# Causal mask of the attention's row maxima: from TensorE products to a fused VectorE instruction

## What is computed

```python
Q, K, V = x @ W_Q.T, x @ W_K.T, x @ W_V.T          # x after layer norm; 16 heads of 16
attn = jnp.einsum('bhqd,bhkd->bhqk', Q, K) * scale
attn = jnp.where(causal, attn, -jnp.inf)
probs = jax.nn.softmax(attn, axis=-1)
y = jnp.einsum('bhqk,bhkd->bhqd', probs, V)
x = x + y @ W_O.T
x = x + ffn(layernorm(x))                          # shared expert and 2 of 16 experts a token
```

## Time and profile before

| | |
|---|---|
| time, median of 3 runs | 857.45 us (856.12 to 858.51) |
| span of the profiled execution | 857.0 us |
| TensorE busy | 750.3 us, 88% |
| TensorE weight loads | 569.0 us, 66% |
| VectorE busy | 523.9 us, 61% |
| ScalarE busy | 401.4 us, 47% |
| GpSimd busy | 359.9 us, 42% |
| granted TensorE clock, mean | 0.951 |

### The profile page before, as it was taken

How to read it: one execution, slowest core, us unless ns; L and a number is a source line. 1 busy time by engine, 2 the same in 40 slices (tenths; PEclk the granted TensorE clock), 3 DMA queues, 4 the chain that set the end, 5 groups by cost and what they waited for, 6 DMA issues and landing times. The chain is left out here.

```text
span 857.0 us, 16360 instructions
## 1 busy us (share of the span) xinstructions
PE 750.3 (88%) x5618; PEld 569.0 (66%) x5619; DVE 523.9 (61%) x1158; ACT 401.4 (47%) x777; POOL 359.9 (42%) x658
## 2 busy tenths in 40 slices
PE   2589899999999999999887587989679999999997
PEld 1355466575666656666454367868579999988886
DVE  6267777677776768766670349445634445456667
ACT  3116656546655556646556132433435556542232
POOL 4305437283472835625374023767700000057771
PEclk9879999999999999999887868999979999999999
DMA  5659366483755738466111221877645555467864
GB/s 148 236 211 321 143 222 224 167 296 130 250 194 209 261 124 282 138 242 228 61 59 51 86 74 62 301 238 240 239 158 155 181 183 160 134 203 242 265 200 137
DMA packets 102500, 159.67 MB, mean 186 GB/s; under 512 B 7712, under 2 KB 78368, under 8 KB 98208
## 3 DMA queue, kind: packets, MB, share of 16 engines
q1 hardware_dynamic: 96288, 141.99, 49.6%
q0 software_dynamic: 6144, 16.79, 5.7%
HBM read 86.66 MB, written 71.83 MB: 185 GB/s over the span
## 5 line engine op out<-in xcount | busy, mean ns | idle before, releaser
L609 DVE TENSOR_REDUCE neg_max<-ps_w 128x1 f32<-128x512 f32 (+3 forms) x352 | 201.0, 633 | 67.5 <-PE ps_w L711 67.3
L546 ACT ACTIVATE probs<-ps_w 128x512 f32<-128x512 f32 x320 | 167.5, 610 | 32.2 <-PE ps_w L724 31.3
L408 POOL TENSOR_TENSOR pool_scratch<-minus_half 1x1 f32<-1x1 f32 x190 | 34.8, 183 | 263.7 <-ACT probs L546 223.6
L1091 POOL DMA_INDIRECT ex<-yg_dram,slots x64 | 64.5, 1009 | 155.6 <-DMA yg_dram<-y 136.4
L438 POOL TENSOR_SCALAR_AFFINE_SELECT probs<-probs 128x256 f32<-128x256 f32 (+1 forms) x224 | 93.7, 429 | 0.0
L1079 POOL DMA_INDIRECT xg_dram<-srow,slots x64 | 68.0, 1063 | 52.2 <-DVE slots L1242 27.4
L735 PE MATMUL ps_w<-probs,v_aug 128*32 128x512 f32 (+3 forms) x1024 | 81.2, 460 | 5.9 <-POOL probs L438 5.8
L191 PE MATMUL ps_f<-stacks 128*128 128x512 f32 x176 | 72.5, 412 | 12.2 <-DVE xT_lo_f L1260 6.8
L1108 ACT ACTIVATE silu<-ps_f 128x512 f32<-128x512 f32 (+1 forms) x48 | 28.5, 594 | 103.7 <-PE ps_f L193 103.7
L192 PE MATMUL ps_f<-xT_lo_f,stacks 128*128 128x512 f32 x176 | 70.9, 403 | 0.0
L193 PE MATMUL ps_f<-stacks 128*128 128x512 f32 x176 | 70.6, 401 | 0.0
(11 more groups left out here) (167 smaller groups left out, 1839.6 us busy)
## 6 DMA issues: line engine op xcount, KB each, us to landing
qk_dram<-projected SPq DMA_DIRECT2D x96, 256.0 KB, 4.3
stacks<-qk_dram SPq DMA_DIRECT2D x16, 1024.0 KB, 6.1
xg_dram<-zeros SPq DMA_DIRECT2D x20, 512.0 KB, 10.5
srow<-xg_dram SPq DMA_DIRECT2D x40, 256.0 KB, 2.8
q_st<-qk_dram SPq DMA_DIRECT2D x8, 1024.0 KB, 4.8
k_st<-qk_dram SPq DMA_DIRECT2D x8, 1024.0 KB, 8.1
projected<-experts SPq DMA_DIRECT2D x16, 384.0 KB, 4.5
yg_dram<-projected SPq DMA_DIRECT2D x20, 256.0 KB, 2.2
```

The lines of the kernel that those rows point to most:

```text
L408: ticks = Ticks(pool, pool_ticks, lambda: pool.tensor_tensor(out=pool_scratch[:, 0:1], in0=minus_half[0:1, 0:1], in1=minus_half[0:1, 0:1], ...
L546: act.activation(probs[:, g, p * PAIR + half * BANK:p * PAIR + (half + 1) * BANK], ps_w[:, plan.bank(kind, which, half), :], ACT.Exp).then ...
L609: dve.tensor_reduce(out=neg_max[u][:, qt, first:first + len(heads)], in_=bank[:, 0:len(heads) * width].rearrange("p (h n) -> p h n", h=len ...
L1091: pool.indirect_dma_start(out=back[:, m, c, :], out_offset=None, in_=yg_rows, in_offset=bass.IndirectOffsetOnAxis(ap=slots[:, c, m:m + 1], ...
```

## The change

The mask products go. `max_pair` ends each half's accumulation with the last product of scores and signals there. A tile `causal` of 128 x 512 fp32 holds zeros in its first 384 columns and -1e30 above the diagonal in its last 128, so that its last `width` columns fit every job. In the step `max` VectorE runs one `tensor_tensor_reduce` a head: it adds the last `width` columns of `causal` to the head's scores, multiplies by -1, writes the result back over the scores in PSUM, and accumulates the minimum, which is the negated maximum. Jobs with two or four heads take two or four of them: 32 a unit, 512 in all, in place of 352 reductions. The two bf16 tiles of the mask product go, GpSimd clears one 128 x 512 tile in their place, and the first maximum waits for it. `max_row` of the two units become slices of one tile.

```diff
-    ident16 = sb("ident16", [P, P], bf16)
-    mask16 = sb("mask16", [P, P], bf16)
+    causal = sb("causal", [P, S], f32)
...
-    max_row = [sb(f"max_row{u}", [HU, S], f32r) for u in range(UNITS)]
+    max_rows_of = sb("max_rows_of", [QUADRANT * (UNITS - 1) + HU, S], f32r)
+    max_row = [max_rows_of[u * QUADRANT:u * QUADRANT + HU] for u in range(UNITS)]
...
-        chain.step(pool.memset(ident16[:, :], 0.0))
-        chain.step(pool.memset(mask16[:, :], 0.0))
+        chain.step(pool.memset(causal[:, :], 0.0))
         chain.wait()
...
-        chain.step(pool.affine_select(out=mask16[:, :], in_=mask16[:, :], compare_op=ALU.is_ge, fill=NEG, base=0,
+        chain.step(pool.affine_select(out=causal[:, S - P:S], in_=causal[:, S - P:S], compare_op=ALU.is_ge, fill=NEG, base=0,
                                       pattern=[[-1, P]], channel_multiplier=1))
...
-                dve.tensor_reduce(out=neg_max[u][:, qt, first:first + len(heads)],
-                                  in_=bank[:, 0:len(heads) * width].rearrange("p (h n) -> p h n", h=len(heads)),
-                                  axis=AX.X, op=ALU.max, negate=True).then_inc(freed["dve"], 1)
+                if which == (0, 0, 0, 0):
+                    dve.wait_ge(pool_chain, 5)
+                for i in range(len(heads)):
+                    scores = bank[:, i * width:(i + 1) * width]
+                    made = dve.tensor_tensor_reduce(out=scores, in0=scores, in1=causal[:, S - width:S], scale=-1.0, scalar=LARGE,
+                                                    op0=ALU.add, op1=ALU.min, accum_out=neg_max[u][:, qt, first + i:first + i + 1])
+                made.then_inc(freed["dve"], 1)
...
-                    pe.matmul(outs[half][:, i * width:(i + 1) * width], q_st[u][b % 2][rows, slot, qt * P:(qt + 1) * P],
-                              k_st[u][b % 2][rows, slot, 0:width], start=i == 0, stop=False)
-
-            for out in outs:
-                blocks = out[:, 0:len(heads) * width].rearrange("p (h n) -> p h n", h=len(heads))[:, :, width - P:width]
-                pe.matmul(blocks, ident16[:, :], mask16[:, :].unsqueeze(1).to_broadcast([P, len(heads), P]), start=False, stop=True)\
-                  .then_inc(work_ready, 1)
+                    made = pe.matmul(outs[half][:, i * width:(i + 1) * width], q_st[u][b % 2][rows, slot, qt * P:(qt + 1) * P],
+                                     k_st[u][b % 2][rows, slot, 0:width], start=i == 0, stop=i == len(heads) - 1)
+                    if i == len(heads) - 1:
+                        made.then_inc(work_ready, 1)
...
-        pe.wait_ge(pool_chain, 7)
+        pe.wait_ge(pool_chain, 5)
```

More of the change, by code:

```diff
@@ L20 @@
 NEG = -1.0e30
+LARGE = 3.0e38
 SCALE = float(DH) ** -0.5
@@ L27 @@
 ROWS = P // HALVES
+QUADRANT = 32
 PART_M = 3
@@ L460, in _ @@
         chain.step(pool.memset(ident[:, :], 0.0))
-        chain.step(pool.memset(ident16[:, :], 0.0))
-        chain.step(pool.memset(mask16[:, :], 0.0))
+        chain.step(pool.memset(causal[:, :], 0.0))
         chain.wait()
-        for m in (ident, ident16):
-            chain.step(pool.affine_select(out=m[:, :], in_=m[:, :], compare_op=ALU.not_equal, fill=1.0, base=0,
-                                          pattern=[[-1, P]], channel_multiplier=1))
-        chain.step(pool.affine_select(out=mask16[:, :], in_=mask16[:, :], compare_op=ALU.is_ge, fill=NEG, base=0,
+        chain.step(pool.affine_select(out=ident[:, :], in_=ident[:, :], compare_op=ALU.not_equal, fill=1.0, base=0,
+                                      pattern=[[-1, P]], channel_multiplier=1))
+        chain.step(pool.affine_select(out=causal[:, S - P:S], in_=causal[:, S - P:S], compare_op=ALU.is_ge, fill=NEG, base=0,
                                       pattern=[[-1, P]], channel_multiplier=1))
```

## The result

| | before | changed |
|---|---|---|
| time, median (lowest to highest, runs) | 857.39 us (856.12 to 858.51, 4) | 880.07 us (877.73 to 885.32, 4) |
| span of the profiled execution | 857.0 us | 877.3 us (its run: 879.05 us) |
| granted TensorE clock, mean | 0.951 | 0.923 |

The changed kernel is slower: ratio 1.0279, 95% interval 1.0246 to 1.0312. The forecast was 870, slower by over 0.3%, with a range of 855 to 910.

The account below looks back on a forecast made before the run. VectorE was taken to bound the stretches where maxima are made, although TensorE is busier overall. Six periods gave +8.1 us, the last batch +1.1, the first +3.1: +12.3 on 857.45, say 870, range 855 to 910.

Parts of the forecast that it names:

- The place: End of the second unit: VectorE's last maximum sets the pace and TensorE, waiting for neg_max, has nothing to give back.
- the wait for GpSimd's selection: First unit, P·V waiting for the diagonal's selection: the 0.76 us of jobs 9 and 10's mask products turn into waiting.
- The read of the accumulator: Second instruction behind each fused one on VectorE, writing one column of neg_max: 512 in all, taken at 0.08 us each.
- r: Cost in VectorE's stream of one accumulator read behind a fused instruction, taken as 0.08 us.
- the MAX8 row: Trace row of four small maxima on VectorE, 0.077 us apart, from which the read's 0.08 us was taken.
- The memset: Trace row of a one-element memset, 0.059 us, listed as a nearest row from below for the read's cost.
- case of r = 0.06: Whole kernel with a cheaper accumulator read: +0.7 us a period and +8 in all, 865 us.
- The width of the columns: VectorE's fused instructions: distance between starts falls by 0.137 us per 128 columns, from 0.60 at 512 to 0.19 at 128.
- The drain: Rival on VectorE: each fused instruction costs its full 0.69 us, reads on top, r 0.17 and above, 908 us; chance 0.22.
- Second unit from the first transposes to VectorE's jobs 4: O additions wait on the oT splits behind four reads and on VectorE itself: +0.17 us a period.
- From there to the end of the maxima: Second unit's end, without cover: idle is eaten and 2.46 us of VectorE work added, +1.3 us a period.
- The first batch: No scores beside its first unit, VectorE alone sets the pace there: +2.1 us, second unit +1.0, together +3.1.

## Why the prediction was right, and where it was not

**The place was right.** The end of the second unit is VectorE's, and TensorE's savings there end in a wait for neg_max (1.91 us). Jobs 9 and 10 at that place carry most of the change's price, as the kernel with only these two undone shows (863.64). In the first unit the savings turned into the wait for GpSimd's selection (0.51 to 1.57), as said: that half fell by 0.3 us, forecast 0.1.

**The read of the accumulator was taken too dear.** Starts lie 0.65, 0.517, 0.383 and 0.249 us apart for 512, 384, 256 and 128 columns (for the last two (188.35 - 186.82) / 4 and (190.34 - 188.35) / 8), against the 0.60, 0.463, 0.327 and 0.19 that the prediction took for the fused instruction alone: r is 0.05 to 0.06, not the 0.08 of the MAX8 row, and at or below the memset's 0.059. The memset was the nearer row. The prediction's own case of r = 0.06 fits the work: it gives +0.7 a period, and +0.65 was measured. For the whole it gives 865, so by r alone the time would have come out 15 us shorter than the 880.07. The width of the columns was right: the steps of 0.137 per 128 columns came out at 0.133 to 0.134. The drain did not come: a fused row of 0.73 us is followed by the next fused row after 0.65. The Trainium skill, page "VectorE: DVE Perf Modes", section "The DRAIN you can't avoid", says that the next operation doesn't start until the pipe is empty, with which these rows don't agree. They agree with the same section's remark that an operation that isn't held starts earlier.

**Term by term, at full clock.** Second unit from the first transposes to VectorE's jobs 4 (163.15 to 178.70 and, in the earlier trace rows, 214.07 to 229.53): +0.1, forecast 0.17. From there to the end of the maxima (178.70 to 190.34, and 229.53 to 240.39): 11.64 against 10.86, +0.8, forecast 1.3. Most of the gap is the smaller r; against it, 0.2 us of idle were left (before 183.12). With the first unit's -0.3 a period grows by 0.65 and not 1.35, six of them by 3.9 and not 8.1. The first batch grew by 1.7 (its end went from 82.14 to 83.86), forecast 3.1. This term can't be checked closely: its first unit ends at 59.51 in the kernel before and already at 57.26 in the one with the wait alone, whose first unit is the same.

**The term that was missing is the clock.** Of the span's +20.3 us, batches 1 to 6 hold 15.9: 3.9 by the work, 12.0 by low clock. The last batch, from 415.80 to 470.27, takes 54.47 instead of 50.79, +3.7 where 1.1 was forecast, and nearly all of it in its first half, at a clock of 0.80 (1.00 before). What follows is 1.0 shorter. 1.7 + 15.9 + 3.7 - 1.0 = 20.3. So the forecast of 870 is 10 us short, and not further off only by luck, since two errors lie in opposite directions: the work cost some 7 us less, and the lower clock, to which the sum gave nothing, some 15 more. (Another 2.4 us lie between the +20.3 of the profiled spans and the +22.7 of the medians.) The prediction had listed the waits for neg_max as a sign to look for, and named no price for what TensorE does behind them. It gave "TensorE busy about 5 us less a period": at full clock it is 49.75 - 44.90 = 4.85.

**What is shown of the clock, and what isn't.** A wait at this place is enough to bring low clock without any other part of the change: put alone into the kernel before, it makes four of six first-unit halves low, and filled with products on the same VectorE path it makes none. That a wait always brings it is not so: two of those six halves keep 1.00, and one in the changed kernel. What decides between them, and whether the gate products behind the wait matter, no run here shows. The Trainium skill, page "TensorE: Matmul & The Clock Gate", section "Part 1: The HAM clock gate (the "warmup" mystery)", has two levels of clock, set by how busy TensorE has been recently. The stretches at 1.00 and at 0.50 agree with the levels, and the kernel with the wait filled (no low half, against four) with the cause. That the wait is the only source is not so either: the changed kernel with the filler, and the one with jobs 9 and 10 undone, have low stretches at other places. The first lacks the mask products, the second most of them, some 5 us of TensorE's work a period, and both kernels that keep them and fill the wait have next to none; that the thinner stream is the cause fits these four. It can't be the whole cause: the three kernels without any mask products but with plain reductions have a stream as thin, and only one or two low halves of twelve. No run here separates it from where the other waits lie.

## What to carry to other kernels

Before work is moved off the busiest engine, ask at each synchronisation which engine arrives last: what is taken from the one that waits is only waited away, and what is added to the last one in front of the wait counts in full (three reductions, 3 x 0.60 us, lengthened each period by 1.8). An instruction that reduces several heads at once should not be split for a fusion: with the narrow shared jobs fused alone the whole loss was there (880.78), with the wide ones alone nearly none (859.02). And ask first whether the work is needed: leaving the mask of the maxima out was the only edit that won, 1.0% (0.9897, 0.9846 to 0.9948).

## What the hardware did that I had not expected

Behind a wait of 1.91 us and sixteen products of 17 columns TensorE's clock was halved in most periods (five of six in the changed kernel, one of them behind 2.78 us), and the greater price is not paid in the wait but behind it: P·V takes 3.7 to 4.5 us instead of 2.36, and the half-period 1.6 to 3.3 us more. Idle work can be faster than idling: eight products that nobody reads took 16.6 us from a kernel with such a wait (879.56 to 862.93, of which 10.6 in the batches concerned), six took 10.3 from another, eight 6 to 8 from the changed one (880.07 and 881.40 to 873.73), and three nothing where the wait was 0.75 us. The fused add and minimum, reading PSUM and SBUF and writing PSUM, runs at nearly the pace of a plain reduction: with its separate accumulator read it takes 0.65 us of the stream for 512 columns, 0.05 more than the reduction, though the read's own row says 0.141.
